# The last chunks' norms, router and table moved beside the first fourteen expert blocks; expert results summed in three groups; pad rows copied in device memory

## What is computed

```python
x = x + xattn(_layernorm(x), ctx)      # 16 heads, softmax over 77 context rows
x = x + ffn(_layernorm(x))
# ffn: xn = layernorm(x)*gamma + beta
#      probs = softmax(xn @ router_w.T / 1.5); w, idx = top_k(probs, 2)     (8 experts)
#      y_e = silu(xn @ W1[e]) @ W2[e]          W1[e]: 128x512, W2[e]: 512x128
#      ffn = x + sum over the two chosen experts of w_e * y_e
```

## Time and profile before

| | us |
|---|---|
| median of 3 runs | 906.27 (904.65 to 907.48) |
| the profiled execution's own time | 900.37 |
| its span, first to last instruction | 898.6 |
| attention until the last sequence is added (DVE, L953) | 503.7 |
| first expert matmul | 568.3 |
| last expert matmul group of M2 ends | about 844.7 |
| last DVE addition ends | 895.4 |

### The profile page before, as it was taken

How to read it: one execution, slowest core, us unless ns; L and a number is a source line. 1 busy time by engine, 2 the same in 40 slices (tenths; PEclk the granted TensorE clock), 3 DMA queues, 4 the chain that set the end, 5 groups by cost and what they waited for, 6 DMA issues and landing times. The chain is left out here.

```text
span 898.6 us, 17277 instructions
## 1 busy us (share of the span) xinstructions
PE 717.1 (80%) x5170; PEld 491.5 (55%) x5170; DVE 618.0 (69%) x2083; ACT 501.9 (56%) x1029; POOL 528.9 (59%) x756
## 2 busy tenths in 40 slices
PE   1799899988989899989998520799989999999500
PEld 1565556655655566556655310577767777777400
DVE  3677678777878786868876433577767777777444
ACT  1476657565747574757665200577767677776300
POOL 6323447776768776877866674056546555565700
PEclk9999979999989997989998755799999999999955
DMA  6544536445544564455442113688888777777287
GB/s 182 118 121 109 140 85 168 103 116 152 165 105 117 153 167 103 111 154 111 94 107 69 33 45 145 207 260 267 259 255 253 225 238 240 229 225 242 88 289 275
DMA packets 153046, 146.58 MB, mean 163 GB/s; under 512 B 53259, under 2 KB 108440, under 8 KB 152920
## 3 DMA queue, kind: packets, MB, share of 16 engines
q1 hardware_dynamic: 141560, 121.59, 48.7%
q0 software_dynamic: 9088, 19.68, 6.4%
q10 hardware_dynamic: 2304, 4.20, 1.2%
HBM read 79.22 MB, written 40.86 MB: 134 GB/s over the span
## 5 line engine op out<-in xcount | busy, mean ns | idle before, releaser
L1269 POOL DMA_INDIRECT ys<-yo,to x156 | 159.6, 1023 | 140.3 <-DVE yo L1154 102.0
L760 ACT ACTIVATE P<-pt 77x512 f32<-77x512 f32 x256 | 152.2, 595 | 111.4 <-PE pt L569 104.9
L1262 POOL DMA_INDIRECT xs<-zz,idx x128 | 131.6, 1028 | 56.8 <-PE ps L556 30.0
L1140 DVE TENSOR_TENSOR sl<-sf,sh 128x512 fp32r<-128x512 f32 x156 | 107.6, 690 | 68.2 <-ACT sh L812 64.7
L931 DVE TENSOR_REDUCE mx<-ps 128x4 f32<-128x308 f32 x256 | 117.7, 469 | 42.0 <-PE ps L556 36.1
L569 PE MATMUL pt<-qd,kc 128*77 128x512 f32 x256 | 116.5, 455 | 14.7 <-DMA qd<-nm 14.4
L580 PE MATMUL po<-P,v 77*9 77x128 f32 x2048 | 107.9, 285 | 3.3 <-ACT osb L768 2.0
L556 PE MATMUL ps<-kd,qc 128*128 128x308 f32 x256 | 101.1, 396 | 4.7 <-DVE mx L931 3.3
L810 ACT ACTIVATE sf<-ps 128x512 f32<-128x512 f32 x78 | 46.7, 599 | 65.2 <-PE ps L492 52.2
L1201 POOL TENSOR_SCALAR ve<-mv 128x4 f32<-128x4 f32 x48 | 11.9, 248 | 102.7 <-DVE mv L845 101.2
L556 PEld LDWEIGHTS ps<-kd,qc 128*128 128x128 f32 x256 | 51.1, 200 | 29.0 <-issue 15.1
(11 more groups left out here) (189 smaller groups left out, 1900.2 us busy)
## 6 DMA issues: line engine op xcount, KB each, us to landing
w<-wsd SPq DMA_DIRECT2D x78, 512.0 KB
qd<-qc SPq DMA_DIRECT2D x128, 128.0 KB
xb<-xs SPq DMA_DIRECT2D x39, 288.0 KB
kd<-kc SPq DMA_DIRECT2D x128, 77.0 KB, 2.3
wsd<-ws SPq DMA_DIRECT2D x8, 1024.0 KB
y<-ys SPq DMA_DIRECT2D x32, 256.0 KB, 4.2
xin<-in_x SPq DMA_DIRECT2D x16, 256.0 KB, 3.7
wr<-in_W SPq DMA_DIRECT2D x16, 256.0 KB
```

The lines of the kernel that those rows point to most:

```text
L760: eng.activation(P[k % 4][:, :], pT[k % 2][0:CS, :], ACT.Exp).then_inc(sems["p"], 1)
L1140: eng.tensor_tensor(sl[k % 6][:, :], sf[k % 3][:, :], sh[k % 6][:, :].bitcast(F), ALU.subtract).then_inc(sems["sl"], 1)
L1262: eng.indirect_dma_start(out=xs, out_offset=at, in_=zz[b][:, j % 4, :], in_offset=None).then_inc(sems[f"sw{b}"], 16)
L1269: eng.indirect_dma_start(out=ys, out_offset=at, in_=yo[u % 2][:, q, :], in_offset=None).then_inc(sems[f"ys{u % 2}"], 16)
```

## The change

Six edits come together.

1. **Order.** TB and the separate expert list are gone. After the attention loop the expert steps are put in the common list, and after each M1 and each M2 step `go()` runs twice, so the side lists lose four entries for each pair M1, M2, 16 for a block. All that was left of norms, routers and scatters (chunk 13's late part, 14 and 15) is thus interleaved with the first expert blocks. The BANKED steps there use only PSUM bank 2 (`late`); YT of the first 14 blocks uses bank 1, which BT uses too.
2. **Two tables.** Counts are taken after chunks 8, 12, 13 and 16 (`COUNTED` = 7, 11, 12, 15 as numbers from zero). Table 1, made during the attention, covers blocks 0 to 13 (`K1` = 14) out of full blocks of rows of chunks 0 to 12, those of chunks 0 to 7 first. Table 2, after chunk 15's router, covers blocks 14 to 38. TN (3 small DVE steps), TA (13 to 18), TM (one PE matmul), TE (3 DVE copies).
3. **Early loads.** Buffer 0 of the rows (`xb0`) and of both weights (`ws`) lie outside the memory that attention uses; BX(0), BW1(0), BW2(0) wait for table 1 and for the scatters of chunks 0 to 12. The second buffers wait for the last attention step.
4. **Register loads.** BX loads four blocks' table entries at a time, rows and experts; BW1 and BW2 load none.
5. **Results.** `yo` has 8 buffers. SA starts in block 6, one per block, two in blocks 13, 17, 21 and 25. Ten of the sixteen CB come in blocks 31 to 38 (one each in 31 to 36, two each in 37 and 38); chunks 0 to 7 wait for blocks up to 27, chunks 8 to 11 for those up to 32, the last four for all.
6. **Pads.** PD, after chunk 15's counts, copies the eight pads from `spare` to `xs` in device memory (no SBUF tile), and nothing before block 14 waits for them.

Besides, thirteen DVE router semaphores become one (`router`), and VP signals once instead of four times.

```diff
 def rows(c):
         for j in range(8):
-            out += [("SW", c, j)] + gap(5 if c < NC - 3 else 0)
+            out += [("SW", c, j)] + gap(5 if c < NC - 4 else 2 if c < NC - 2 else 0)
...
+    def table(k):
+        return ([("TA", k, j) for j in range(13)] + gap(3) + [("TM", k), ("TE", k)] + [("TA", k, j) for j in range(13, 18) if k == 1])
+
+    def counted(c):
+        i = COUNTED.index(c)
+        return ([("PD",)] if c == NC - 1 else []) + [("TN", i, j) for j in range(3)] + {NC - 4: table(1), NC - 1: table(2)}.get(c, [])
...
-    while tails[0] or tails[1]:
-        go()
-    put(("TB",))
-    while tails[2]:
-        go()
+    for step in expert_steps():
+        put(step)
+        if step[0] in ("M1", "M2"):
+            go()
+            go()
...
 def expert_steps():
-    out = [("BX", 0), ("BW1", 0), ("BW2", 0), ("BX", 1), ("BW1", 1), ("BW2", 1), ("BX", 2), ("BT", 0)]
+    out = [("BX", 0), ("BW1", 0), ("BW2", 0), ("BW1", 1), ("BW2", 1), ("BX", 1), ("BX", 2), ("BT", 0)]
+    summed = {31: [0], 32: [1], 33: [2], 34: [3], 35: [4], 36: [5], 37: [6, 8], 38: [7, 9]}
...
-        if f == 1 and 0 <= u - 2 < NBLK:
-            out.append(("SA", u - 2))
-            if rest:
+        if f == 1:
+            for _ in range(0 if u < 6 else 2 if u in (13, 17, 21, 25) else 1):
+                if sent < min(u - 1, NBLK):
+                    out.append(("SA", sent))
+                    sent += 1
+            if u >= 2 and rest:
...
+        if f == 3:
+            out += [("CB", j, c) for j, c in enumerate(sum(summed.values(), [])) if c in summed.get(u, [])]
...
-        xb = tile(sb, "xb", [128, 4, ROW], F, 3)
+        xb = [xb0] + tile(sb, "xb", [128, 4, ROW], F, 2)
+        w1 = ws[:, 0:2, :], tile(sb, "w1o", [128, 2, 512], R)[:, :, :]
+        w2 = ws[:, 2:4, :], tile(sb, "w2o", [128, 2, 512], R)[:, :, :]
...
+            def PD():
+                w.wait_ge("padi", 1)
+                for at in many(padi, 0, E, E * AREA - BLK):
+                    load(xs[bass.ds(at, BLK), :].rearrange("(p q) w -> p (q w)", p=128),
+                         spare[0:BLK, :].rearrange("(p q) w -> p (q w)", p=128), "pads")
             def BX(u):
+                if u not in at_row:
+                    w.wait_ge("tab", 1 if u < K1 else 2)
+                    top = min(u + 4, K1 if u < K1 else NBLK)
+                    at_row.update(zip(range(u, top), many(offi, u, top, E * AREA + (E - 2) * BLK)))
+                    at_exp.update(zip(range(u, top), many(ebi, u, top, E - 1)))
+                    for s in range(2):
+                        w.wait_ge(f"sw{s}", 128 * ((NC - 2 - s) // 2 if u < K1 else NC // 2))
+                    if u >= K1:
+                        w.wait_ge("pads", 16 * (E + 1))
+                if u == 1:
+                    w.wait_ge(*freed("PR", NB - 1))
                 w.wait_ge("bT", u - 2)
                 w.wait_ge("w8", u - 2)
-                at = eng.value_load(offi[0:1, u:u + 1], min_val=0, max_val=E * AREA + (E - 2) * BLK)
...
-            def CB(c):
-                w.wait_ge(f"so{c % 4}", 16 * (c // 4))
-                for s in range(2):
-                    w.wait_ge(f"ys{s}", 64 * ((NBLK + 1 - s) // 2))
+            def CB(j, c):
+                k = j % 4
+                w.wait_ge(f"so{k}", 16 * (j // 4))
+                last = K1 + 13 if c < 8 else K1 + 18 if c < 12 else NBLK - 1
+                for s in range(NYO):
+                    w.wait_ge(f"ys{s}", 64 * ((last - s) // NYO + 1))
...
             def YT(u):
-                w.wait_ge("pm2", taken_a[2])
-                w.wait_ge("yo", u)
+                if u < K1:
+                    w.wait_ge("xnb", u + 3)
+                else:
+                    w.wait_ge("pm2", taken_a[2])
+                    w.wait_ge("yo", u)
```

More of the change, by code:

```diff
@@ L96, in put @@
                 tails[2] += gap(3) + rows(step[1])
+            if step[:1] == ("TP",) and step[2] == 13 and step[1] in COUNTED:
+                tails[3] += counted(step[1])
     def go():
@@ L193, in expert_steps @@
             out.append(("BX", u + 3))
-    return out + [("CB", c) for c in range(NC)]
+        if f == 3:
+            out += [("CB", j, c) for j, c in enumerate(sum(summed.values(), [])) if c in summed.get(u, [])]
+    done = sum(summed.values(), [])
+    out += [("SA", u) for u in range(sent, NBLK)]
+    return out + [("CB", j, c) for j, c in enumerate(done + list(range(len(done), NC))) if j >= len(done)]
 def xattn_moe(nc, x, ctx_in, qw, qb, kw, kb, vw, vb, pw, pb, gam, bet, rwT, W1, W2, ident, sel, one24, iota, cst, tok, spare, out):
@@ L324, in xattn_moe @@
         uses, taken_a = bank_uses(order)
-        steps_b = expert_steps()
+        before = bank_uses(order[:order.index(("BT", 0))])[1]
         flat = lambda t: t[:, :, :].rearrange("p a b -> p (a b)")
@@ L422, in WS, with many @@
                     load(wsd[e_].rearrange("a p w -> p a w"), ws[:, :, :].bitcast(F), "wst")
-            def TB():
+            def many(src, lo, hi, top):
+                return list(nc.values_load_multi_w_load_instructions(src[0:1, lo:hi], engines=[mybir.EngineType.SP], min_val=0,
+                                                                     max_val=top)[1])
+            def PD():
                 w.wait_ge("padi", 1)
-                for e_ in range(E):
-                    at = eng.value_load(padi[0:1, e_:e_ + 1], min_val=0, max_val=E * AREA - BLK)
-                    load(xs[bass.ds(at, BLK), :].rearrange("(p q) w -> p (q w)", p=128), flat(pad), "pads")
-                w.wait_ge("pads", 16 * (E + 1))
-                for s in range(2):
-                    w.wait_ge(f"sw{s}", 128 * (NC // 2))
-                    w.wait_ge(f"sx{s}", 16 * (NC // 2))
-                w.wait_ge("wst", 16 * E)
-                w.wait_ge("tab", 2)
@@ L661, in M2 @@
                 if k == 0:
-                    w.wait_ge("pm0", taken_a[0])
+                    w.wait_ge("pm0", before[0])
                     w.wait_ge("osb", NB)
```

380 lines of the change are left out of this document (224 added, 156 removed).

## The result

The changed kernel takes 923.17 us (median of 4 runs, 921.25 to 924.34), the kernel before 905.46 us beside it (4 runs, 900.26 to 907.48): a ratio of 1.0203, 95% interval 1.0155 to 1.025. It is slower; the prediction was 841 us. The profiled execution took 921.25 us for a span of 919.4.

What follows compares the result with a forecast made beforehand. Bound by PE for 39 expert blocks, a serial chain ahead of them and DMA behind: 900.4 - 59.3 + 15 + 5 - 4 + 1.5 + 7 - 30.2 = 835.4, plus 5.9 to the median: 841 us, range 820 to 864.

Steps and rivals of the forecast that it cites:

- The hole: Between last attention sum and first expert matmul: matmul at 507.0 instead of 568.3, -61.3; with +2 for late rows, -59.3.
- the signs: Expected profile: first expert matmul at 506 to 509; wrong if expert part much over 300 us or PE starts after 515.
- Attention, +1.5: During attention: table 1's small DVE steps, more count matmuls and a table matmul on nearly full PE cost 0 to 3.
- The tail: After the last M2: ten sums moved away, so 23.7 us instead of 53.9, -30.2.
- POOL, "Cost 0, covered by the empty blocks": POOL's 33.2 us from before the experts fit under blocks 0 to 9, with result scatters kept from blocks 0 to 5.
- Sums under the last blocks, +7: Blocks 31 to 38: DVE waits for sum loads and PE behind it, 3 to 20 us, taken as +7.
- What moves under the experts, +15, range to +30: Early expert blocks: PE's own work 5.3, waits 7, table loads 3, together +15; range +6 to +30.
- Pads, +5, range 0 to 13: Block 7.3, SP's queue: pad copies of 2.36 MB hold up weight loads by 0 to 13 us, taken as +5.
- Register loads, -4, range -7 to +6: SP in expert blocks: weights issued 1.5 to 2.5 us earlier, but each fourth block 1 to 2 later; taken as -4.
- Table loads: ACT under the experts: exp twice among silus, four table loads of 1.28 us, 5.1 in all; six in the whole kernel.
- D: Slower than before: DVE waits at each early sum for crowded, growing landings, above 23 us; over 906.3, some 915; chance 0.02.
- rival B: Expert part bound by something else: pads 10, register loads +6, interleaving 30, sums 20; 889, or 865; 856 to 900, chance 0.16.

Runs made afterwards that it cites:

- the void edit with groups of four: Changed kernel, all sums at the end; scatters of four blocks placed together from block 26, which left POOL's order unchanged: 850.16 us on a kind II chip.

## Why the prediction was wrong, point by point

- **The hole.** Right. The first expert matmul came at 510.1, 1.6 us over the forecast with its attention term, and 1.1 past the 506 to 509 of the signs; the late report of the next point is more than that.
- **Attention, +1.5.** The last attention sum ended at 507.8 instead of 503.7, +4.2, and the cause is again a late report. The fifth sum from the end began at 484.7, 3.4 us earlier than in before; the next one came 11.3 us behind it, against 4.4 in before. Between the two POOL issued eight scatters of chunk 12 in a row (482.7 to 492.6), which have two empty entries between them in the new list where there were five. ScalarE's `P` answers a matmul that ended at 487.1 only at 494.2, and PE waits for it:

```profile
486.61 0.46 PE L618 MATMUL pt<-qd,kc 128*77 128x512 f32 x1
...
491.63 0.96 POOL L1367 DMA_INDIRECT xs<-zz,idx  x1 [0.30 <-issue]
494.18 0.59 ACT L818 ACTIVATE P<-pt 77x512 f32<-77x512 f32 x1 [7.24 <-remote]
...
494.82 0.71 PE L618 MATMUL pt<-qd,kc 128*77 128x512 f32 x1 [5.52 <-ACT P L818]
```

This step takes 9.9 to 11.3 us in all eight traces of this attention part on kind I and 4.8 to 6.7 in the seven on kind II. Beside it stands the clock, which changes from execution to execution: the first `gl` lies between 503.9 and 517.8 us on kind I, and between 489.7 and 508.8 on kind II. These are the windows of 300 to 400 in two versions with the same attention part, on two chips of kind II (first the void edit with groups of four, whose first `gl` stands at 489.7; then the changed kernel, 506.0), columns as in the earlier trace rows:

```profile
300.00:400.00 100.00, 92.39 (x839) 57.74 (x840) 81.19 (x337) 62.65 (x141) 76.21 (x125) 0.97 0.49 131
```

```profile
300.00:400.00 100.00, 93.08 (x782) 57.82 (x781) 76.61 (x316) 60.17 (x134) 72.04 (x117) 0.88 0.47 127
```

PE is as busy in both, and gets 839 and 782 matmuls done, at a granted clock of 0.97 and 0.88. What the term priced, table 1's small steps, can't be told beside these two.

- **The tail.** Right: 23.73 us measured, 23.7 forecast. That it agrees to the tenth is luck: the last scatter landed 11.3 us behind the last M2 (forecast 10.2), and the rest took 12.5 (forecast 13.5).
- **POOL, "Cost 0, covered by the empty blocks".** This is the step that failed worst. I priced POOL's indirect transfers as time of POOL, and found room for it. They did have room. But the same plan made POOL issue 16 and then 28 of them without a pause, beside PE at work; and on kind I that holds back TensorE's reports to ScalarE and VectorE. 32 us of the miss (blocks 7 and 10: 20.7 + 38.2 against 9.4 + 17.3 on kind II, and against 9.5 + 16.6 with pauses on kind I), and some 6 more in attention, as said above. The trace of before could hardly have warned of it: in its expert part POOL pauses after every four but for one run of seven and the twelve at its end, and its two long runs lie where PE is mostly idle.
- **Sums under the last blocks, +7.** The mechanism was half seen. I counted VectorE's stand at the landing, and gave PE three steps in hand. I overlooked that CB stands in ScalarE's list too, and that a store there waits for VectorE's sum, with `sf` and `sh` of the next blocks queued behind it. ScalarE stood 47.8 us in 7 waits, and the sums cost 33 us by the run without them: the term was mis-sized by 26 to 28. With each engine's part one block after its supplier's, and the last two sums behind the blocks, they cost 1 to 2 us (blocks 33 to 38 on kind II: 42.9 and 43.5 us, against 41.7 to 41.9 with all sums at the end).
- **What moves under the experts, +15, range to +30.** On kind II blocks 1 to 10 take 99.1 us, against 66.5 in before: +32.7, of which 6.8 are PE's wait behind the pads, so some 26, inside the range; 2 of them belong to the first point, so the term was mis-sized by 9. PE is busy for 77.1 us there against 63.9, at a granted clock of 0.88 against 0.96. The waits were others than forecast: for `mcum` and the like PE stood under 2 us in all, but 6.2 in 7 places for `yo` ahead of BT, which shares a bank with YT in these blocks (edit 1; not in the sum), and 5.1 in 4 places for `yT`.
- **Pads, +5, range 0 to 13.** PE's wait behind them is 5.3 to 9.0 us in 13 of the 15 traces of a changed kernel (the other two list none), 7.5 in the changed kernel itself: mis-sized by up to 4. The rule of the Trainium skill that I weighed there, on the page "DMA: Bandwidth & Descriptors", "Queues, rings and completion order" (descriptors of a queue are consumed in ring order), pointed to the upper end; the wait of 7.5 us for `ws` behind the copies agrees with it, at about half of the 13.
- **Register loads, -4, range -7 to +6.** Wrong sign. Blocks 11 to 32 cost 11.4 us more, with peaks at 14, 18, 22, 26 and 30: each fourth block, where SyncE has all eight at once ahead of its loads; the blocks with two SA (13, 17, 21, 25) stand next to the first four of these, but not to 30. PE waited 11.3 us for `w1o` in 5 places, of which one of 3.7 lies in block 10, against 7.7 in 9. The price for those blocks was in the text as an upper end, +6, and was nearer than the value taken. No run changes the register loads alone, so that they are the cause is argued from the place of the peaks.
- **Table loads.** Six in the whole kernel, as forecast, 1.28 us each as in before. The Trainium skill names a further drain of about 1380 ns in "ScalarE: Activation LUTs", "What ACT_TABLE_LOAD costs". The trace of the changed kernel does not have it: at its four switches under the experts ScalarE's activations stand 0.02 us ahead of the load and 0.01 to 0.02 us behind it (538.83 to 538.85, the load to 540.13, the next `sf` at 540.14). So a switch costs 1.3 us there, and 5.1 to 5.2 for the four, as the sum had it.
- **The sum.** Late reports 32.2; the sums 35.2 (27.5 + 7.7, all that the last rows of the table hold) for 7, so 28.2; blocks 1 to 10 otherwise 30.3 (12.8 + 49.7 - 32.2) for 22 (15, 5 and 2), so 8.3; blocks 11 to 32 at +11.4 for -4, so 15.4. Together 84.1, and but for rounding the whole of the expert part's miss of 84.2. On kind II the first falls away and the same kernel takes 864 and 879 us, where before takes 878: a gain of 65 us, as forecast, is far off even there.
- **Rivals.** The outcome, slower than before, was D's, with a chance of 0.02. In mechanism rival B came nearest: the terms that it raised did come out higher (interleaving some 24 for its 30, pads 5 to 9 for 10, registers +11 for +6, sums 33 for 20), but it had no term for the reports. D named the place of the second loss, and a mechanism (landings above 23 us) that isn't the one: the landings stayed at about 5 us (median 5.3), and it was the order of the lists that made them count.

## What to carry to other kernels

Where one engine's list holds both the work of the inner loop and a step that waits for another engine's slow chain, put that step a block later than its supplier's, on every engine that has a part in it; ten sums cost 33 us in one place of the lists, and eight of them, cut in three, a block apart, cost 1 to 2. When work is moved from a stretch where the bound engine is idle to one where it is busy, ask what it does to that engine other than taking time: here runs of GpSimd transfers that did no harm beside an idle TensorE cost 32 us beside matmuls, on some chips. And an edit of order changes nothing unless a wait or a neighbour in that engine's list changes with it: look at the list of the one engine first.

## What the runs showed of the hardware that I had not expected

- On some chips (before: 900 to 906 us) an unbroken run of indirect transfers from GpSimd, one every 1.27 us, delays what TensorE reports to ScalarE and VectorE. The first late report came 4.4, 9.3 and 8.0 us into the three runs of the changed kernel's trace and 9.1 us into the run that was made on purpose; reports come 3 to 12 us late, the last of them at about the end of the run. A pause of 0.9 us after every four transfers removes nearly all of it (ScalarE's `sf`: 39.9 to 3.3 us), breaks of 0.1 us after two do not. Six transfers a block instead of four cost 110 us over the blocks from the fourth on, twice, of which GpSimd's own time explains 30.
- On other chips (before: 876 to 878 us) 60 in a row did nothing, and the same kernels are 2 to 7% faster. Which of two versions is faster depends on the chip: the changed kernel with its sums at the end is at 1.0091 of before (1.004 to 1.0142) on the first kind and at 0.9815 (0.9693 to 0.9936) on the second. What differs in the chips, and by what path a transfer of GpSimd touches TensorE's reports, the runs don't show.
